# Cross attention: the folds of two heads on 64 array rows each, three products per fold, and all eight heads of a half in one run

## The reference

```python
q = (query @ Wq + bq).reshape(b, sq, 16, 64)       # query: layer norm of x
k = (key @ Wk + bk).reshape(b, 256, 16, 64)        # key = value = context
v = (value @ Wv + bv).reshape(b, 256, 16, 64)
scores = einsum('bqhd,bkhd->bhqk', q, k) / 8
out = einsum('bhqk,bkhd->bqhd', softmax(scores), v) @ Wo + bo + query
x = x + layernorm(out) * gamma + beta
```

## Time and profile before

| | before |
|---|---|
| median of three runs | 2145.27 us (2142.52 to 2146.36) |
| span of the profiled execution (the page gives it no other time) | 2145.9 us |
| granted TensorE clock, mean of the span | 0.993 |
| TensorE matmul busy | 2097.1 us (98%) |
| TensorE weight load busy | 1850.5 us (86%) |
| VectorE busy | 1568.1 us (73%) |
| ScalarE busy | 1271.4 us (59%) |
| POOL busy | 946.7 us (44%) |
| fold matmuls (L976) | 1024, 299 ns and 284 ns in the mean, overlapping |

### The profile page before, as it was taken

The page is one execution under the profiler, slowest core; times in us unless marked ns, Lnnn a source line. Parts: engine busy times, 40 slices in busy tenths (PEclk is TensorE's granted clock), DMA queues, the critical chain, the costliest instruction groups (busy, mean ns, idle before and its releaser), DMA issues.

```text
span 2145.9 us, 46808 instructions
## 1 busy us (share of the span) xinstructions
PE 2097.1 (98%) x15864; PEld 1850.5 (86%) x15865; DVE 1568.1 (73%) x2774; ACT 1271.4 (59%) x3067; POOL 946.7 (44%) x800
## 2 busy tenths in 40 slices
PE   8999999999999999999999999899998999999997
PEld 7898899899899888888898998678886888888886
DVE  7667767767767677677677676699996877666665
ACT  5566666656656665666656666377774335555553
POOL 5323322322333332233223223288884234777775
PEclk9999999999999999999999999999999999999999
DMA  5000000010010010000100100255533222333332
GB/s 156 11 21 25 24 20 24 10 34 20 15 34 20 15 34 15 20 24 10 34 24 10 34 10 1 63 160 158 166 117 101 87 73 56 55 54 53 54 54 42
DMA packets 100687, 103.91 MB, mean 48 GB/s; under 512 B 11953, under 2 KB 90161, under 8 KB 100625
## 3 DMA queue, kind: packets, MB, share of 16 engines
q1 hardware_dynamic: 86992, 84.47, 12.6%
q0 software_dynamic: 13632, 18.62, 5.4%
HBM read 72.52 MB, written 30.54 MB: 48 GB/s over the span
## 4 chain that ended last, share of the span: by engine, by line
PE 76%; POOL 10%; issue 6%; DVE 4%; ACT 2%; DMA 2%; POOLq 0%; DVEq 0%; ACTq 0%
PE banks L933 38%; PE banks L976 6%; PE banks L1006 5%; PE banks L1021 5%; PE banks L1034 5%; POOL out_dram L2434 4%; PE banks L1675 3%; POOL r_x L2398 3%; PE banks L2273 2%; POOL index L2405 2%; DMA out_dram<-r_y,index 2%; PE banks L1738 1%; PE banks L963 1%; PE banks L1697 1%; PE banks L1754 1%
## 5 line engine op out<-in xcount | busy, mean ns | idle before, releaser
L933 PE MATMUL banks<-ctxT_hi,qk_hi 128*128 128x256 f32 x1024 | 300.2, 293 | 0.0
L933 PE MATMUL banks<-ctxT_hi,qk_lo 128*128 128x256 f32 x1024 | 289.1, 282 | 0.0
L933 PE MATMUL banks<-ctxT_lo,qk_hi 128*128 128x256 f32 x1024 | 286.8, 280 | 0.0
L567 ACT ACTIVATE probs<-banks,nbias 128x256 f32<-128x256 f32 x512 | 236.9, 488 | 77.7 <-DVE nbias L700 77.3
L453 POOL TENSOR_TENSOR rinv<-rsum,inverse 128x4 f32<-128x4 f32 x96 | 96.8, 1008 | 396.8 <-ACT probs L567 396.8
L574 ACT ACTIVATE pc<-banks 128x512 f32<-128x512 f32 x256 | 153.3, 599 | 190.9 <-PE banks L933 187.8
L658 DVE TENSOR_TENSOR qk_lo<-banks,qk_hi 128x512 fp32r<-128x512 f32 x256 | 163.6, 685 | 87.9 <-ACT qk_hi L529 87.8
L695 DVE TENSOR_REDUCE peak<-banks 128x4 f32<-128x1024 f32 x128 | 156.3, 1221 | 80.0 <-PE banks L933 80.0
L933 PE MATMUL banks<-pT_hi,ctx_hi 128*128 128x512 f32 x512 | 205.1, 401 | 1.7 <-DVE pT_lo L658 1.7
L658 DVE TENSOR_TENSOR pT_lo<-banks,pT_hi 128x512 fp32r<-128x512 f32 x256 | 164.4, 683 | 57.1 <-ACT pT_hi L529 56.6
L933 PE MATMUL banks<-pT_hi,ctx_lo 128*128 128x512 f32 x512 | 202.2, 395 | 0.0
(11 more groups left out here) (271 smaller groups left out, 6165.7 us busy)
## 6 DMA issues: line engine op xcount, KB each, us to landing
ctx_raw<-in_ctx_dram SPq DMA_DIRECT2D x64, 256.0 KB, 2.7
experts_w<-in_L_ffn_We_dram SPq DMA_DIRECT2D x24, 512.0 KB, 4.0
x_in<-in_x_dram SPq DMA_DIRECT2D x16, 256.0 KB, 2.8
x_again<-in_x_dram SPq DMA_DIRECT2D x16, 256.0 KB, 2.8
x_stream<-z SPq DMA_DIRECT2D x16, 256.0 KB, 2.1
s_x<-x_stream SPq DMA_DIRECT2D x32, 128.0 KB, 3.8
s_x_again<-x_stream SPq DMA_DIRECT2D x32, 128.0 KB, 3.2
x_normalised<-s_xl SPq DMA_DIRECT2D x32, 128.0 KB, 1.7
```

Source lines behind the costliest of these rows:

```text
L567: nc.scalar.activation(probs[:, s % 2, p, :], scores[:, s % 2, p // 2, (p % 2) * SK:(p % 2 + 1) * SK], ACT.Exp, bias=nbias[:, s % 2, p:p + ...
L933: last = nc.tensor.matmul(out, a, b, start=(n == 0), stop=(n == 3 * len(pairs) - 1))
```

## The change

Queries get a tile for each part, `q_hi` and `q_lo`, with two heads on the 128 partitions; they are written by two 128-partition instructions per bank on each of the two engines. The key weights are held once, head 2p on partitions 0 to 63 and head 2p + 1 on 64 to 127; they are transposed in half as many pieces. The small load of `bq_low` goes. A fold of two heads is twelve matmuls: for each 128 output rows the three products, and for each product one matmul on array rows 0 to 63 into one bank and one on rows 64 to 127 into another. In steps 3 and 7 all eight heads are folded in one run, then come both part products, and in step 7 the qbk product behind them; ScalarE and VectorE follow the same order. The two score banks of even steps count as banks 4 and 5 of the ring and take heads 0, 1, 6 and 7. The fold waits for the exponentials of the step before, and the first scores of the next half wait for heads 6 and 7. Some banks of steps 3 and 7 change.

```diff
 RING = 4
+BANKS_USED = RING + 2
...
         if b == 3:
-            for i in range(HALF // 2):
-                c = part_of_pc(i)
-                if i == 0 and (g.cur if half else g.prev):
-                    out.append(("o", half))
-                if g.cur and c is not None:
-                    out.append(("pc", s, c))
-                if s == 7 and g.next and i == 3:
-                    out.append(("qbk",))
-                if (g.next if half else g.cur):
-                    out += [("fold", half, h) for h in (2 * i, 2 * i + 1)]
+            folds = g.next if half else g.cur
+            if g.cur if half else g.prev:
+                out.append(("o", half))
+            if folds:
+                out += [("fold", half, h) for h in range(HALF)]
+            if g.cur:
+                out += [("pc", s, c) for c in range(DC)]
+            if s == 7 and g.next:
+                out.append(("qbk",))
...
-    ("pc", 3): (0, 2), ("pt", 3): (0, 3), ("pc", 4): (2, 0), ("pt", 4): (3, 1),
+    ("pc", 3): (1, 2), ("pt", 3): (0, 3), ("pc", 4): (2, 0), ("pt", 4): (3, 1),
...
-    ("pc", 6): (3, 0), ("pt", 6): (1, 3), ("pc", 7): (2, 3), ("pt", 7): (0, 1),
-    ("fold", 0): (1, 2, 3, 1, 0, 3, 1, 2), ("fold", 1): (1, 3, 0, 1, 2, 0, 3, 2),
+    ("pc", 6): (3, 0), ("pt", 6): (1, 3), ("pc", 7): (1, 3), ("pt", 7): (0, 2),
+    ("fold", 0): (4, 5, 1, 2, 0, 3, 4, 5), ("fold", 1): (4, 5, 1, 3, 2, 0, 4, 5),
 }
-SINGLE_BANKS = {"ctxT": (1, 2, 2, 2), "o": (3, 0), "wk": (0, 1, 0, 1), "xT": (3,), "qbk": (1,), "qbk0": (3,)}
+SINGLE_BANKS = {"ctxT": (1, 2, 2, 2), "o": (3, 0), "wk": (0, 1), "xT": (3,), "qbk": (2,), "qbk0": (3,)}
...
-            for hp in range(2):
-                for i in range(2):
-                    pair = target * PAIRS + 2 * m + i
-                    last = nc.scalar.activation(
-                        q_st[0:DK, 4 * m + 2 * i + hp, :], bank[DK * hp:DK * hp + DK, i * GT:(i + 1) * GT],
-                        ACT.Identity, bias=bq[DK * hp:DK * hp + DK, pair:pair + 1])
-                last.then_inc(hi_done, 1)
+            for i in range(2):
+                pair = target * PAIRS + 2 * m + i
+                last = nc.scalar.activation(q_hi[:, 2 * m + i, :], bank[:, i * GT:(i + 1) * GT], ACT.Identity,
+                                            bias=bq[:, pair:pair + 1])
+            last.then_inc(hi_done, 1)
...
+            if b == 0 and not (g.kind == 0 and s == 0):
+
+                for h in (HALF - 2, HALF - 1):
+                    wait_freed(pe, g, ("fold", 1 - half, h), half - 1)
...
-                bank, done = bank_for(pe, g, ("fold", half, h))
+                if g.kind != -1 and p % 2 == 0:
+
+                    pe.wait_ge(exp_done, PAIRS * (STEPS * g.at + half * GB + GB - 1))
+                to = [bank_for(pe, g, ("fold", half, 2 * p + e)) for e in range(2)]
                 for c in range(DC):
-                    for n, w in enumerate((wk_hi, wk_lo)):
-                        last = nc.tensor.matmul(bank[:, c * GT:(c + 1) * GT],
-                                                w[:, target * HALF + h, c * P:(c + 1) * P], q_st[:, h, :],
-                                                start=(n == 0), stop=(n == 1))
-                last.then_inc(done, 1)
+                    for n, (w, v) in enumerate(((wk_hi, q_hi), (wk_hi, q_lo), (wk_lo, q_hi))):
+                        for e, (bank, done) in enumerate(to):
+                            rows = slice(e * DK, (e + 1) * DK)
+                            ins = nc.tensor.matmul(bank[:, c * GT:(c + 1) * GT],
+                                                   w[rows, target * PAIRS + p, c * P:(c + 1) * P], v[rows, p, :],
+                                                   start=(n == 0), stop=(n == 2))
+                            if c == DC - 1 and n == 2:
+                                ins.then_inc(done, 1)
```

More of the change, by code:

```diff
@@ L258, in cross_attention @@
     x_reloaded = sem("x_reloaded")
-    filled = [sem(f"filled{k}") for k in range(RING)]
-    freed = [sem(f"freed{k}") for k in range(RING)]
+    filled = [sem(f"filled{k}") for k in range(BANKS_USED)]
+    freed = [sem(f"freed{k}") for k in range(BANKS_USED)]
     hi_done = sem("hi_done")
@@ L284, in cross_attention, with bank_at @@
     bank_turns = [Turns(lambda kind, k=k: [key for key in ring_order(kind) if ring_bank(key, kind) == k], -1, GROUPS)
[L285 to L289, removed]
+                  for k in range(BANKS_USED)]
+    SPLIT = ("ctxT", "xT", "fold", "pt", "wk", "q")
+    hi_turns = Turns(lambda kind: [key for key in ring_order(kind) if key[0] in SPLIT], -1, GROUPS)
+    def bank_at(k):
+        return ring[:, k, :] if k < RING else scores_banks[:, k - RING, :]
     def place(g, key, groups_on=0):
@@ L620, in scalar @@
                 if b == 3:
-                    for i in range(HALF // 2):
-                        c = part_of_pc(i)
-                        if g.cur and c is not None:
+                    folds = g.next if half else g.cur
+                    if folds:
+                        for h in range(HALF):
+                            fold_upper(g, half, h)
+                    if g.cur:
+                        for c in range(DC):
                             copy_pc(g, s, c)
-                        if (g.next if half else g.cur):
-                            for h in (2 * i, 2 * i + 1):
-                                fold_upper(g, half, h)
                 elif (g.cur if s >= 2 else g.prev):
@@ L673, in q_lower @@
             target = 1 - half
[L674 to L681, removed]
+            dve.wait_ge(hi_done, nth_hi(g, ("q", half, m)))
+            for i in range(2):
+                pair = target * PAIRS + 2 * m + i
+                last = nc.vector.scalar_tensor_tensor(
+                    out=q_lo[:, 2 * m + i, :], in0=ring[:, k, i * GT:(i + 1) * GT], scalar=bq[:, pair:pair + 1],
+                    in1=q_hi[:, 2 * m + i, :], op0=ALU.add, op1=ALU.subtract)
             last.then_inc(freed[k], 1)
@@ L856, in vector @@
                 if b == 3:
[L857 to L866, removed]
-                        if (g.next if half else g.cur):
-                            for h in (2 * i, 2 * i + 1):
-                                fold_lower(g, half, h)
+                    folds = g.next if half else g.cur
+                    if s == 7 and g.cur:
+                        dve.wait_ge(resid_done, g.at + 1)
+                        add_o(g, half, resid)
+                    if s == 3 and g.prev:
+                        wait_freed(dve, g, ("o", 1), -1)
+                        add_o(g, half, z)
+                    if folds:
+                        for h in range(HALF):
+                            fold_lower(g, half, h)
+                    if s == 7 and g.next:
+                        keep_qbk(g)
                 if b == 2 and (g.next if half else g.cur):
@@ L914, in tensor, with wk_pairs @@
     def tensor(pe):
-        def wk_heads(bank, h):
-            for e in range(2):
+        def wk_pairs(bank, pair):
+            for i in range(2):
                 for c in range(DC):
-                    for low in range(2):
-                        last = nc.tensor.matmul(
-                            bank[low * DK:(low + 1) * DK, (e * DC + c) * P:(e * DC + c + 1) * P],
-                            wk_raw[:, c, (h + e) * DK:(h + e + 1) * DK], ident[:, :], start=True, stop=True)
+                    last = nc.tensor.transpose(bank[:, (i * DC + c) * P:(i * DC + c + 1) * P],
+                                               wk_raw[:, c, (pair + i) * P:(pair + i + 1) * P], ident[:, :])
             return last
@@ L1108, in tensor @@
                 if g.kind == 0 and s == 3:
-                    for i in range(4):
+                    for i in range(2):
                         wait_freed(pe, g, ("wk", i))
@@ L1119, in tensor @@
                 if b == 3:
-                    for i in range(HALF // 2):
-                        c = part_of_pc(i)
-                        if i == 0 and (g.cur if half else g.prev):
-                            do_o(g, half)
-                        if g.cur and c is not None:
-                            do_pc(g, s, [c])
-                        if s == 7 and g.next and i == 3:
-                            do_qbk(g)
-                        if (g.next if half else g.cur):
-                            do_fold(g, half, (2 * i, 2 * i + 1))
+                    folds = g.next if half else g.cur
+                    if g.cur if half else g.prev:
+                        do_o(g, half)
+                    if folds:
+                        do_fold(g, half, range(PAIRS))
+                    if g.cur:
+                        do_pc(g, s)
+                    if s == 7 and g.next:
+                        do_qbk(g)
                 elif (g.cur if s >= 2 else g.prev):
```

86 lines of the change are left out of this document (36 added, 50 removed).

## The result

The changed kernel takes 2164.5 us (median; 2162.9 to 2166.9) against 2144.8 for the kernel before beside it (2142.5 to 2146.4): ratio 1.009, 95% interval 1.0078 to 1.0102. It is 19.7 us slower, where 4.2 were forecast; the sign and most of the places were right, the size was not.

The account below looks back on a forecast made before the run. TensorE's own stream was taken to bound the kernel. Fifteen groups of 0.69 - 0.14 give +8.3 us, start and q -4.0, so the span of 2145.9 becomes 2150.2 and the time 2149.5 (+0.2%); range 2137 to 2185.

Parts of the forecast that it names:

- Rival A: Fold couples run one matmul at a time, 0.18 or more per couple: slower, 2198 us; chance 0.13.
- Rival C: POOL's context split slows VectorE's qbk instructions in step 7: +0.7 us in each of 15 groups, 2160; chance 0.17.
- The matmuls: Fold runs: two matmuls on different array row halves run together, 0.119 us per couple, 24 couples 2.86.
- Entering and leaving: Switching TensorE into and out of tiles at each fold run: 0.15 us in, 0.20 out.
- Rival B: Cheap tile switches: no drain and 0.103 to 0.107 us per couple, faster, 2135 us; chance 0.20.
- The evacuation wait: Fold run: fourth pair waits until VectorE has lowered heads 0 and 1; 0.84 us lost, run complete at 3.85.
- Step 3: Per steady group: run +0.23 us, part products same, transposes 0.87 instead of 1.24; -0.14 in all.
- Step 7: Per group: run +0.14 us and wait for the qbk bank +0.55; +0.69 in all.
- The qbk wait: Step 7: second transpose group waits for VectorE to empty bank 2, complete at Q + 1.42 against Q + 0.87: +0.55 us.
- Start and q: Kernel start, 2.3 us less from fewer weight transposes, splits and loads, with the q part's saving: together -4.0 us.
- The q part: Eight 64-partition instructions become four of 128 on both engines; worth 1.7 us, only in group 0 where TensorE waits.
- The sum: Whole kernel: fifteen groups +8.3 us, start and q -4.0; profiled span 2145.9 becomes 2150.2, time 2149.5, or +0.2%.

Follow-up runs that it names:

- experiment 4: Changed kernel with the fourth pair of heads in banks of their own (heads 6 and 7) and the qbk product in bank 1: 2118.8 us, ratio 0.9869.
- experiment 6: Changed kernel's tiled folds in the order and four banks of the kernel before, pairs of heads between part products: 2166.2 us, ratio 1.0093.
- Experiment 3: Changed kernel with heads 6 and 7 in banks of their own, step 7's exponentials ahead of the folds on ScalarE: 2139.7 us, ratio 0.9966.
- experiment 1: Changed kernel with step 7's qbk product in bank 1 instead of bank 2, nothing else: 2149.1 us, ratio 1.0008.
- experiment 5: Kernel before, full-array folds without tiles, with all eight heads in one run, six banks, qbk last in bank 1: 2142.0 us, ratio 0.9976.
- experiment 8: Experiment 4 with the small load of the query bias's low rows (bq_low) put back: 2115.2 us, ratio 0.986.
- experiment 2: Changed kernel with the two banks of step 7's transposes exchanged, so the first group waits for bank 2: 2166.2 us, ratio 1.0087.
- experiment 7: Experiment 4 with 24 idle transposes ahead of group 0's wait for POOL's weights: 2117.0 us, ratio 0.9868.

## Why the prediction went as it did, step by step

The measured 2164.5 lies inside the stated range (2137 to 2185), but above the forecast's own (2141 to 2157). It is inside through the room that was kept for rivals A and C, and neither happened; that much is luck. A steady group was to grow by about 0.5 us and grew by 1.29.

**The matmuls: right.** A couple of 64*128 costs one pitch, 0.119. Rival A (0.18 and more) is refuted.

**Entering and leaving: right in sum.** 0.20 in where 0.15 was taken (experiments 4 and 6); out 0.16 (a run's part products 2.96 against 2.80) to 0.19 (experiment 6) where 0.20 was taken. Rival B, cheap switches, is refuted; the gaps of the earlier trace rows are paid at each run, as the Trainium skill's rule on mode switches (TensorEngine Tiling (Array Packing), Key Properties) says.

**The evacuation wait: right.** Forecast were a loss of 0.84 and a run of 3.85. The couples stand 0.95 apart where 0.12 is a pitch, so 0.83 is lost, and the run takes 3.99. The 0.14 more are 0.05 on entry and 0.09 in the first couple after the wait, which takes 0.39 and not 0.28. Experiment 3 takes this wait away and leaves the one on qbk.

**Step 3: right, mis-sized by 0.10.** 3.99 + 2.96 + 0.87 = 7.82 instead of the 7.72 that the forecast's terms make and of 7.86 before.

**Step 7: the term that failed.** To the end of the first scores matmul it takes 9.01 before and 10.20 after (525.09 to 535.29), +1.19 where +0.69 was forecast. The run and its exit are +0.25 (forecast +0.14). The qbk wait is right: the second transpose group is complete 1.46 behind the qbk product, forecast 1.42, against 0.87. The other +0.35 is the loop turn (0.32 of it), which the forecast did not have: I took the wait to end with the transposes, and did not ask what TensorE must do next with an empty queue. It comes 13 times, not 14 as the expectation of experiment 1 has it: 4.2 us at 0.32 each. In all the two steps make 1.19 - 0.04 = 1.15 per group; the measured 1.29 leaves 0.14, 2 us.

These lie in steps 2 and 6. From one step's first scores matmul to the next step's, step 2 takes 13.18 instead of 13.10 and step 6 14.13 instead of 14.02. Most of step 2's part is in its 24 query projection matmuls, which the change does not touch: they start 0.120 apart instead of 0.117. Every run without the tile `bq_low` has the 13.18, every run with it (before, experiments 5 and 8) the 13.10, and experiment 8, which is experiment 4 with this tile and its load put back, has a group of 82.23 instead of 82.38. The tile takes 64 bytes of each partition and moves those allocated after it; that their place is the cause is not shown. In step 6 a further 0.07 goes with qbk in bank 2.

**Rival C: wrong.** POOL's split runs 532.89 to 534.18 beside the qbk instructions, and these take what they took in the earlier trace rows:

```profile
532.89 1.29 POOL L435 TENSOR_TENSOR ctx_lo<-ctx_raw,ctx_hi 128x512 fp32r<-128x512 f32 x1
...
533.31 0.73 DVE L706 SCALAR_TENSOR_TENSOR qbk<-banks,wqb 64x16 f32<-64x16 f32 x4 [1.77 <-PE banks L915]
```

**Start and q: -4.0 forecast, -1.0 measured in one profile.** Experiments 1 and 2 have the same code up to group 0's projection of step 7 and reach it at 94.9 and 93.5, so the -1.0 is uncertain by 2 us, and the start is short of -4.0 in all three. The q part did what was said: the wait of 2.2 for it is 1.2, and between the first scores after step 1's transposes (38.94, before 38.45) and those after step 2's (49.76, before 51.03) the changed kernel gains 1.76, forecast 1.7. In this profile the start brings nothing. This is the changed kernel's chain of waits there, from the first qbk product to step 1's transposes:

```profile
28.06 2.75 PE banks L915 x12
...
31.67 1.24 DVE peak L682
...
34.39 1.94 ACT probs L559 x8
...
36.57 1.24 DVE probs L718
...
37.85 1.09 PE banks L998 x8
```

And the kernel before, same view:

```profile
35.53 1.90 PE banks L921 x32
37.42 1.02 PE banks L1006 x8
```

Before, TensorE's own stream reached 37.42. With 1.9 us of it taken out, step 0's softmax is late instead: 7.04 us from the end of the qbk product (30.81) to the transposes, and the saving becomes a wait. The product itself starts 1.1 earlier, not 2.8, since POOL's weights end at 28.02 instead of 26.33: its product starts 0.66 later, and its five additions take 3.36 once and 3.14 once, beside VectorE instructions on SBUF alone, instead of 2.30. Before, one product took 2.16 instead of 1.28 in the same company; 0.66 + 1.06 + 0.85 - 0.88 = 1.69 is the whole delay. TensorE has waited 2.5 us for them and is then at half clock (granted 0.50 from 28 to 32 us), which is why twelve small matmuls take 2.75; in experiment 4, at full clock, they take 1.51 (27.61 to 29.12). Last, group 0's step 3 gives back 0.5: its transposes start 0.78 earlier than before, after scores 1.27 earlier, because the fourth pair waits 3.2 there. Group 0's folds stand behind the exponentials on ScalarE, so heads 0 and 1 are freed late (58.08). With banks of their own (experiment 4) those transposes start at 59.98 instead of 63.69; that is the earlier start that its expectation lacked, and experiments 3, 7 and 8 have it too (the projection at 91.0, 90.9 and 92.9).

**The sum.** Fifteen groups bring 18.7 instead of 8.3, and the start -1.0 instead of -4.0; after the last group's projection of step 7, 0.9 come back that the forecast did not have, which leaves the span's 16.8. The terms that failed are the loop turn, which was missing, and the start.

## What to carry to other kernels

Once matmuls are packed so that a bank fills faster than it is emptied, count in banks: a run of heads costs what the evacuation of a reused bank costs. Lending two more banks at the right moment was worth 1.60 us per group, and without it the packing, worth 1.20 when nothing waits, brought a loss. A product that is consumed at once must not share its bank with the next group in line. Look at what stands between the last wait and a loop's back edge; moving the wait forward hid the turn in experiment 2, but the longer wait ate the gain, and only removing the wait paid (experiment 1). And, when a stream that bounds a start gets shorter, price the latency chain that lay just under it.

## What the runs showed of the hardware that was not expected

- A loop turn showed as 0.32 us on TensorE when four 128-column transposes stood between the last wait and the loop's end, and as under 0.1 with eight (0.90 from the first of them to the next scores); behind a tiled run it showed as 0.25 with eight and no wait (experiment 6). The compare-and-branch lasts 0.21 in the median.
- Row-tiled couples with full 128-column loads stream at 0.119 us per couple, 0.20 to enter and 0.16 to 0.19 to leave; the first couple after a wait lasts 0.39 instead of 0.28.
- POOL's five 128x256 additions took 2.29 to 2.31 us, also beside VectorE instructions that read PSUM, and 3.14 to 3.36 beside VectorE instructions on SBUF alone (L694, L696 and L641 of the changed kernel), while four VectorE instructions that read PSUM kept 0.73 beside POOL's product.
- The same full-array projection matmuls stood 0.117 us apart in kernels with a 64-byte tile more in SBUF and 0.120 in those without it.
